# Layer norm of the last two batches with channels on the partitions: token statistics as rows by way of DRAM, in place of transposes on TensorE

## The reference

```python
xn = (x - mean(x)) / sqrt(var(x) + 1e-5)        # over the channels
q, k, v = xn @ wq.T, xn @ wk.T, xn @ wv.T       # 16 heads of q, 4 of k and v, 128 wide; rope on q and k
s = lightning_attention(q, k, v) @ wo.T         # linear attention with decay
h = silu((xn @ q8(gate_w)) * gate_scale) * ((xn @ q8(up_w)) * up_scale)    # 1536 wide, q8 rounds to fp8 e4m3
g = silu((h @ q8(down_w)) * down_scale)
out = x + s * g
```

## Time and profile before

| | us |
|---|---|
| three runs | 907.12, 908.81, 908.90; median 908.81 |
| profiled execution | 907.59 |
| its span | 905.8 (granted clock 0.999) |
| PE busy | 889.8, 98% of the span |
| DVE busy | 631.0, 70% |
| ACT busy | 421.7, 47% |
| POOL busy | 373.0, 41% |

### The profile page before, as it was taken

One profiled execution on the slowest core, in us unless ns is written; L12 is line 12 of the kernel. 1 busy time (PEld: TensorE's weight loads), 2 busy tenths in 40 slices (PEclk: granted clock), 3 DMA queues, 4 the chain that ended last, 5 costly groups with the idle time before them and its releaser, 6 DMA issues.

```text
span 905.8 us, 12411 instructions
## 1 busy us (share of the span) xinstructions
PE 889.8 (98%) x4104; PEld 738.4 (82%) x4104; DVE 631.0 (70%) x903; ACT 421.7 (47%) x709; POOL 373.0 (41%) x276
## 2 busy tenths in 40 slices
PE   5999999999999999999999999999999999999997
PEld 4888888888788888888888888888888888888886
DVE  7777652676753256766777867677767677788797
ACT  3633443443533446345464444464544554634542
POOL 1011112121222475535456455364454563553547
PEclk9999999999999999999999999999999999999999
DMA  6793304477750624414333413144243143364482
GB/s 213 222 360 115 105 12 152 150 256 288 289 219 29 209 93 137 177 33 154 138 118 140 178 67 140 52 182 185 81 162 123 39 171 141 102 236 152 156 266 76
DMA packets 51115, 138.55 MB, mean 153 GB/s; under 512 B 4224, under 2 KB 25344, under 8 KB 45696
## 3 DMA queue, kind: packets, MB, share of 16 engines
q1 hardware_dynamic: 51072, 138.00, 43.1%
HBM read 96.04 MB, written 41.94 MB: 152 GB/s over the span
## 4 chain that ended last, share of the span: by engine, by line
PE 85%; issue 5%; POOL 4%; DVE 3%; DMA 2%; ACT 1%; POOLq 0%; SPq 0%; DVEq 0%; ACTq 0%
PE bank L1268 84%; POOL d_r L1204 2%; POOL rot L1213 1%; DMA v_decayed<-vd_split 1%; PE bank L1315 1%; DMA stage<-in_x_nat 0%; DVE tail_sb L1110 0%; PE bank L1424 0%; DVE vd_split L882 0%; DVE d_sb L1013 0%; DVE tail_sb L1112 0%; ACT gout L547 0%; DVE tail_sb L1096 0%; DVE acc L1106 0%; DVE stats L772 0%
## 5 line engine op out<-in xcount | busy, mean ns | idle before, releaser
L1268 PE MATMUL bank<-xn,aw 128*128 128x512 f32 x960 | 229.2, 390 | 0.0
L1213 POOL TENSOR_TENSOR rot<-rot 128x512 f32<-128x512 f32 x80 | 126.8, 1585 | 235.2 <-DVE rot L1000 235.2
L1268 PEld LDWEIGHTS bank<-xn,aw 128*128 128x128 f32 x960 | 179.0, 188 | 37.4 <-issue 0.7
L1268 PE MATMUL bank<-o_r,ow 128*128 128x512 f32 (+1 forms) x792 | 186.2, 385 | 0.0
L1204 POOL TENSOR_TENSOR d_r<-d_sb,d_r 128x512 fp32r<-128x512 f32 x127 | 166.8, 1337 | 37.0 <-ACT d_r L691 36.9
L1268 PE MATMUL bank<-xn,gu_w 128*128 128x512 f32 x768 | 179.9, 389 | 0.0
L1268 PEld LDWEIGHTS bank<-xn,gu_w 128*128 128x128 f32 x768 | 144.1, 188 | 30.1
L1268 PEld LDWEIGHTS bank<-o_r,ow 128*128 128x128 f32 x792 | 144.4, 188 | 28.5
L999 DVE TENSOR_TENSOR rot<-bank,rope 128x512 f32<-128x512 f32 x80 | 55.2, 690 | 103.2 <-ACT rot L671 103.2
L670 ACT COPY rot<-bank 64x512 f32<-64x512 f32 x80 | 46.8, 585 | 155.1 <-PE bank L1268 154.8
L691 ACT CAST d_r<-d_sb 128x512 fp32r<-128x512 f32 x128 | 79.0, 621 | 84.0 <-DVE d_sb L1059 61.6
(11 more groups left out here) (82 smaller groups left out, 943.9 us busy)
## 6 DMA issues: line engine op xcount, KB each, us to landing
xn<-xn_split SPq DMA_DIRECT2D x15, 2048.0 KB, 7.7
v_decayed<-vd_split SPq DMA_DIRECT2D x32, 512.0 KB, 3.4
vd_r<-v_decayed SPq DMA_DIRECT2D x16, 1024.0 KB, 7.0
v_r<-v_split SPq DMA_DIRECT2D x16, 512.0 KB, 5.6
wst<-in_mlp_w SPq DMA_DIRECT2D x10, 768.0 KB, 5.4
xn_split<-xn SPq DMA_DIRECT2D x3, 2048.0 KB, 10.7
stage<-in_attn_w SPq DMA_DIRECT2D x4, 1280.0 KB, 6.0
stage<-in_x_nat SPq DMA_DIRECT2D x16, 256.0 KB, 4.7
```

What stands on the lines that cost most here:

```text
L1213: pool.tensor_tensor(rot1[:, r % RRING, :], rot1[:, r % RRING, :], rot2[:, r % RRING, :], ALU.add).then_inc(qk_sum, 1)
L1268: last = pe.matmul(dst, a, b, start=start and x == 0, stop=stop and x == len(pairs) - 1)
```

## The change

Batches 0 and 1 stay as they are. For batches 2 and 3 the natural tiles are still loaded and their statistics taken. The columns of mean and rstd are then written to DRAM as rows (`store_rows`: two DMAs, in which every 4-byte element goes to a place of its own), x is loaded again as four tiles of `x_t` (128 channels x 512 tokens, 256 KB each), and the two rows are read back, each to all 128 partitions (`load_rows`: two DMAs of 256 KB on the SBUF side). DVE subtracts the mean row and multiplies by the rstd row, two instructions for each of the 4 tiles; ACT rounds the high part and DVE subtracts the low one, as before but out of SBUF.

SP: store_rows(2) and load_rows(2) stand behind the last weight load; store_rows(3) stands in (2, 2), load_rows(3) in (2, 5). The natural tiles 14 and 15 are loaded once the first two turned tiles of batch 2 are used up. spill_last moves from (2, 8)..(2, 11) to (2, 10), (2, 11), (3, 0), (3, 1), and the attention weights' load from (2, 8) to (2, 10). DVE and ACT: the normalising of batch 2 moves from slabs 6 to 10 to slabs 10 and 11, that of batch 3 from (2, 2)..(2, 7) to (2, 7), (2, 8) and (2, 9).

```diff
+SPILL_AT = [(2, 10), (2, 11), (3, 0), (3, 1)]
+NAT = [i % XRING for i in range(3 * TT)] + [4, 5, 0, 1]
+TURNED = {2: [0, 1, 2, 3], 3: [2, 3, 4, 5]}
...
+        rows = gout[:, 0:2, :]
...
+            def store_rows(s):
+
+                sp.wait_ge(rstd_d, s + 2)
+                i0, i1 = s * TT, s * TT + TT
+                sp.dma_start(row_dram[s - 2, 0].rearrange("t p -> p t"), mv[:, i0:i1, 0], allow_slow_non_contiguous=True).then_inc(row_out, 16)
+                sp.dma_start(row_dram[s - 2, 1].rearrange("t p -> p t"), rstd[:, i0:i1], allow_slow_non_contiguous=True).then_inc(row_out, 16)
+                for k in range(KT):
...
+                    sp.dma_start(stage[:, TURNED[s][k], :], x_t[k, :, bass.ts(ORDER[s], S)]).then_inc(xt_in[k], 16)
+
+            def load_rows(s):
...
+                sp.wait_ge(row_out, 32 * (s - 1))
+                for r in range(2):
+                    row = row_dram[s - 2, r].rearrange("t p -> (t p)")
+                    sp.dma_start(rows[:, r, :], row.unsqueeze(0).broadcast_to([P, S])).then_inc(row_in, 16)
...
             for m in range(6, MT):
                 load_w(m)
+            store_rows(2)
+            load_rows(2)
             for i in range(3 * TT, 4 * TT):
                 load_x(i)
             spill_xn(2)
...
+            def norm_t_hi(s, k):
+
+                act.wait_ge(scaled, (s - 2) * KT + k + 1)
...
+                act.copy(xn_of(s)[:, 0, k, :], stage[:, TURNED[s][k], :]).then_inc(ln_hi, 1)
...
-                if m in (6, 7):
-                    norm(2 * TT + 2 * (m - 6))
-                    norm(2 * TT + 2 * (m - 6) + 1)
-                if 7 <= m < 7 + TT:
-                    norm_hi(2 * TT + m - 7)
+                if m in (MT - 2, MT - 1):
+                    norm_t_hi(2, 2 * (m - MT + 2))
+                    norm_t_hi(2, 2 * (m - MT + 2) + 1)
...
+            def norm_t(s, ks):
+
+                dve.wait_ge(row_in, 32 * (s - 1))
+                c = (s - 2) * KT
+                for k in ks:
+                    dve.wait_ge(xt_in[k], 16 * (s - 1))
+                    xt = stage[:, TURNED[s][k], :]
+                    dve.tensor_tensor(xt, xt, rows[:, 0, :], ALU.subtract).then_inc(centred, 1)
+                for k in ks:
+                    dve.wait_ge(centred, c + k + 1)
+                    xt = stage[:, TURNED[s][k], :]
+                    dve.tensor_tensor(xt, xt, rows[:, 1, :], ALU.mult).then_inc(scaled, 1)
...
-                if 7 <= m < 7 + TT:
-                    norm_lo(2 * TT + m - 7)
+                if m in (MT - 2, MT - 1):
+                    norm_t(2, (2 * (m - MT + 2), 2 * (m - MT + 2) + 1))
+                if m == MT - 1:
+                    norm_t_lo(2, 0)
+                    norm_t_lo(2, 1)
                 fuse(1, m)
+            norm_t_lo(2, 2)
+            norm_t_lo(2, 3)
...
-                    if s == 2 and LND <= m < LND + TT:
-                        norm_lo(3 * TT + m - LND)
+                    if s == 2 and m in (7, 8):
+                        norm_t(3, (2 * (m - 7), 2 * (m - 7) + 1))
+                    if s == 2 and m in (8, 9):
+                        norm_t_lo(3, 2 * (m - 8))
+                        norm_t_lo(3, 2 * (m - 8) + 1)
...
-                if 7 <= m < 7 + TT:
-                    ln_transpose(2 * TT + m - 7)
...
-                    if s == 2 and LND <= m < LND + TT:
-                        ln_transpose(3 * TT + m - LND)
```

More of the change, by code:

```diff
@@ L224, in attention_mlp_kernel @@
         floor_c = sem("floor_c"); newton = sem("newton"); rstd_d = sem("rstd_d")
+        row_out = sem("row_out"); row_in = sem("row_in"); xt_in = [sem(f"xt_in{k}") for k in range(KT)]; centred = sem("centred"); scaled = sem("scaled")
         normed = sem("normed"); ln_t = sem("ln_t"); ln_hi = sem("ln_hi"); ln_lo = sem("ln_lo")
@@ L255, in ln_ps @@
         def ln_ps(i):
-            return bank[i % TT] if i < 2 * TT else bank[7]
+            return bank[i % TT]
         def ready(m, down=False):
@@ L288, in load_x @@
             def load_x(i):
-                if i >= XRING:
-                    sp.wait_ge(ln_t, i - XRING + 1)
-                sp.dma_start(stage[:, i % XRING, :], x_nat[ORDER[i // TT], :, i % TT, :]).then_inc(x_in[i % XRING], 16)
+                if i >= 3 * TT + 2:
+                    sp.wait_ge(ln_lo, 2 * TT + NAT[i] + 1)
+                elif i >= 3 * TT:
+                    sp.wait_ge(stats_d, i - 1)
+                elif i >= XRING:
+                    sp.wait_ge(ln_t, i - XRING + 1)
+                sp.dma_start(stage[:, NAT[i], :], x_nat[ORDER[i // TT], :, i % TT, :]).then_inc(x_in[NAT[i]], 16)
+            def store_rows(s):
[4 more added lines that the diff above has]
+                for k in range(KT):
+                    if s == 2:
+                        sp.wait_ge(ln_t if k < 2 else stats_d, 2 * TT if k < 2 else 2 * TT + k - 1)
+                    else:
+                        sp.wait_ge(ln_lo if k < 2 else stats_d, 2 * TT + k + 3 if k < 2 else 3 * TT + k - 1)
+                    sp.dma_start(stage[:, TURNED[s][k], :], x_t[k, :, bass.ts(ORDER[s], S)]).then_inc(xt_in[k], 16)
+            def load_rows(s):
+                if s == 2:
+                    for r in range(2):
+                        sp.wait_ge(v_out[r], 32 * (2 * TT // VFIRST))
+                else:
+                    sp.wait_ge(gate_out, 16 * KT)
+                sp.wait_ge(row_out, 32 * (s - 1))
+                for r in range(2):
+                    row = row_dram[s - 2, r].rearrange("t p -> (t p)")
+                    sp.dma_start(rows[:, r, :], row.unsqueeze(0).broadcast_to([P, S])).then_inc(row_in, 16)
             def load_piece(q):
@@ L386, in _ @@
                         store_vd(*VD_AT[s, m])
+                    if s == 2 and m == 2:
+                        store_rows(3)
+                    if s == 2 and m == 5:
+                        load_rows(3)
                     if s == 2 and m in (3, 5, 7, 9):
                         fetch_v((m + 1) // 2)
[L389 to L392, removed]
+                    if (s, m) in SPILL_AT:
+                        spill_last(SPILL_AT.index((s, m)))
+                    if (s, m) == SPILL_AT[0]:
+                        sp.wait_ge(ln_lo, NB * TT)
                         sp.dma_start(stage[:, 0:PT, :], attn_w[0]).then_inc(aw_in, 16)
@@ L633, in _ @@
                         v_round(VT_AT[s, m])
-                    if s == 2 and m in (2, 3):
-                        norm(3 * TT + 2 * (m - 2))
-                        norm(3 * TT + 2 * (m - 2) + 1)
-                    if s == 2 and LND <= m < LND + TT:
-                        norm_hi(3 * TT + m - LND)
+                    if s == 2 and m in (7, 8):
+                        norm_t_hi(3, 2 * (m - 7))
+                        norm_t_hi(3, 2 * (m - 7) + 1)
                     if s == 3 and AW_FROM <= m < AW_FROM + PT:
@@ L770, in tile_stats @@
             def tile_stats(i):
-                dve.wait_ge(x_in[i % XRING], 16 * (i // XRING + 1))
-                dve.bn_stats(stats[:, i, :], stage[:, i % XRING, :]).then_inc(stats_d, 1)
+                dve.wait_ge(x_in[NAT[i]], 16 * (NAT[:i].count(NAT[i]) + 1))
+                dve.bn_stats(stats[:, i, :], stage[:, NAT[i], :]).then_inc(stats_d, 1)
             def mean_var(grp):
@@ L809, in norm_lo, with norm_t_lo @@
                 dve.tensor_tensor(lo, ln_ps(i)[:].rearrange("p (k c) -> p k c", k=KT), hi.bitcast(F32),
+                                  ALU.subtract).then_inc(ln_lo, 1)
+            def norm_t(s, ks):
[9 more added lines that the diff above has]
+                    dve.tensor_tensor(xt, xt, rows[:, 1, :], ALU.mult).then_inc(scaled, 1)
+            def norm_t_lo(s, k):
+                dve.wait_ge(ln_hi, s * TT + k + 1)
+                dve.tensor_tensor(xn_of(s)[:, 1, k, :], stage[:, TURNED[s][k], :], xn_of(s)[:, 0, k, :].bitcast(F32),
                                   ALU.subtract).then_inc(ln_lo, 1)
@@ L1301, in v_tile @@
                     pe.wait_ge(ln_lo, v + TT)
+                    pe.wait_ge(v_lo, v)
                 else:
```

13 lines of the change are left out of this document (5 added, 8 removed).

## The result

The changed kernel took 919.94 us, the median of 4 runs (918.18 to 920.50), against 908.41 for the kernel before in the same comparison: ratio 1.0131, 95% interval 1.0118 to 1.0143. It is 11.5 us slower. The forecast was 905.8, so the size, the sign and the range were all missed. The profiled execution took 920.5 us, the slowest of the four, with a span of 918.7; that of the kernel before was 0.8 us under its median, so the two traces lie 12.9 us apart.

A forecast was written before the change was run, and what follows sets the result against it. PE, busy 98% of the span, was taken as the bound. 907.59 - 3.5 (transposes) - 0.5 (old gates wait) + 1.0 (new stall) = 904.6 for the profiled execution; median 905.8 us, range 904.3 to 907.2.

The forecast's parts named there:

- Batch 3, the DMA side: Row stores and 1 MB of x_t added in (2, 2) fit its free DMA time, 3.7 us; lag taken as 0.
- What covers the new work of batch 2: Before slab 10, some 29 us cover batch 2's row stores and loads; 4 us per row store, nothing on the path.
- rival D: Rows come late for batches 2 and 3 if a 4-byte element takes 0.5 us; +4, 912.8 us; chance 0.04.
- Nothing to 2 us of lag, taken as 0.: Delay of the stores of decayed v, next in (2, 3), from row stores and x_t loads added in (2, 2).
- rival C: Side chain of ACT, DVE and landings becomes the bound by (3, 0): 6.5 us stall, +2.5, 911.3 us; chance 0.08.
- the signs set down beforehand: Right: row stores landing under 10 us, among others. Wrong: PE waiting over 2 us together for silu or v_rest, among others.
- The second term: v_rest(12) behind the gates of (3, 0), its preceding store now behind the weights' load: 0 us taken, up to 2.
- -3.5 us for the transposes: PE loses the 32 transposes of batches 2 and 3, 8 x 0.44 us on the chain: 3.5 us less.
- the start of batch 2 without a wait: DVE's last low half done at 147.65, 0.9 us before PE needs it; 0 taken, with 0 to 0.5.
- the gates of (3, 0): PE waits for ACT's gates in (3, 0): a stall of 1.0 us in place of 0.5 now.
- The forecast's engine part: DVE's added batch 3 work in (2, 7) to (2, 9) delays ACT's silus, giving a 1.0 us PE stall at the gates.
- The v for (2, 7): 0.5 MB of row loads before fetch_v(3) in (2, 5) delay this v by 1.5 us; DVE starts (2, 7) at 201.

The follow-up runs named there:

- e2: Kernel before with only the two 4-byte row stores of batch 3 added in (2, 2), read by nobody; 911.91 us, ratio 1.0041.
- e12: Changed kernel with rows packed into 4 DMAs of 8 pieces, and spill_last and weights' load moved late, to (3, 0) to (3, 3); 907.02 us, ratio 0.9992.
- e11: Changed kernel with rows packed into 4 DMAs of 8 pieces, without DVE's four mean subtractions for batch 3; 911.16 us, ratio 1.0031.
- e10: Changed kernel with packed rows, late spill and weights, batch 3's x_t loads in (2, 0), rows in (2, 1), norm_t in (2, 3), (2, 4); 904.27 us.
- e1: Changed kernel without the two row stores of batch 3, which then uses batch 2's rows; 912.93 us, ratio 1.0047.
- e4: Changed kernel with batch 3's two row stores issued by ACT on its own queue at the end of (2, 2); 920.36 us, ratio 1.0134.
- e13: Kernel before with two unread 2 KB stores added in (2, 2), each 128 pieces of 16 B; 908.00 us, ratio 0.9999.
- e8: Changed kernel with mean and rstd packed and turned by DVE, rows leaving as 4 DMAs of 8 pieces of 128 B; 912.16 us, ratio 1.0053.
- e3: Changed kernel without batch 3's four x_t loads (1 MB), row stores kept; 916.67 us, ratio 1.0086.
- e9: Changed kernel with packed rows, late spill and weights, batch 3 normalised in (2, 4), (2, 5), its rows read back in (2, 2); 908.70 us, ratio 1.0015.

## Why the prediction was wrong

**The step that failed** is "Batch 3, the DMA side", with the price put into it under "What covers the new work of batch 2". I took 4 us for a row store, with 6.3 (the scales, 128 pieces of 112 B) as the upper bound; it is 11, outside both ends. The bounds came from rows with as many pieces (v_split, 512 B each) or with small pieces (the scales), and neither has pieces of 4 B. What the Trainium skill says in the place quoted there (DMA: Bandwidth & Descriptors, Rules for kernel authors and Specifications), one descriptor for each element and a read-modify-write below 512 B, was the right warning. The traces agree with the first (1023 packets recorded for the 1024 elements of e2); no run here shows the second. I let the warning count only where the rows could come late (rival D), not where they stand in front of others. Rival D's measure, landing time over the pieces on an engine, gives 11 / 64 = 0.17 us, under its edge of 0.28, and batch 2 did not wait: rows issued at 102.0, read back from 114.5, DVE's norm_t at 130.6.

In (2, 2) the same 11 us met the stores of decayed v. I had found 3.7 us free in that window and "Nothing to 2 us of lag, taken as 0."; the next store was 13 us under way and ACT waited 12.6 us. From there the course was rival C's (given 0.08): ACT's lag beyond the slack of the banks. It put 6.5 us of stall; there were 11.2, and 4.1 of slow clock on top, a term that no case of mine had. The forecast looked at waits of PE and forgot that a wait of 5.2 us can also slow what follows. Of the signs set down beforehand, one of being right failed (row stores landed in under 10 us), and one of being wrong came: PE waited 10.4 us for silu and v_rest, against 2.

**The second term** was v_tile(13), "0, up to 2": 3.2 us and 1.7 of slow clock; without the row stores even 4.4 and 2.2. I had named the mechanism (the weights now stand in front of the store) and priced it by the slack of before, not by the slack that the lag of (2, 7) to (2, 9) left. The chain of before was misread as well: 217.55 in the earlier trace rows is where the late store begins, and it landed 8.16 later, at 225.7.

**Right were:** -3.5 us for the transposes (slabs 7 to 10 take 9.07 us each in the profile after, as forecast); the start of batch 2 without a wait (last low half done at 147.4, PE there at 147.9; two meetings with POOL behind 139, I had counted one and a margin of 0.9); and, in part, the gates of (3, 0) at 0.8 for 1.0. In the changed kernel that wait came behind ACT's 12.6 us for a store and two longer stalls, which the forecast did not have, so the number there is luck; but e12, with the 12.6 us gone, still has 0.6 there and 1.3 at the silus, behind DVE's norm_t as forecast. The forecast's engine part was right in kind and put 1.0 us where 1.9 stand. How much of the rest is DVE's list of 26 to 31 us is not separated: e11 takes a third of the new work away and shows at most 1 us, and e10 moves the loads along with the work. The v for (2, 7) came in e1 at 203.5 and not at 201, behind the row loads, where I had 1.5 us of delay counted.

## What to carry to other kernels

A small DMA is not priced by its bytes: look at its pieces, and measure one with the same size of piece. The price can be paid by whoever comes behind it, on any queue, and a free DMA engine in the profile does not show that the way is free. Turn 4-byte columns on chip first. When two moves each fit into the slack of a chain, check them together: the burst was free in the kernel before and cost 5 us behind a lag of 4. Allow for slow clock behind a forecast stall of PE of some us: here it was 1.6 to 2.9 us behind nine of eleven stalls of 2.8 to 5.3 us, and nothing behind the other two. A list that fits into its slabs on average can still hold up an engine that waits for it in order, as norm_t did. Put together, coarse rows gave 7.8 us back, the late burst 5.1 and the earlier place of batch 3's work and loads 2.7.

## What the runs showed of the hardware

- Two DMAs of 512 pieces of 4 B (2 KB each) from SBUF to DRAM land in 9.6 to 12.0 us. Until they have landed, what is issued behind them soon moves slowly: 26 GB/s in e2 from 183 to 187 where the kernel before moves 347, 98 in the changed kernel from 177.5 to 186. Issued from ACT (e4), they hold up SP's stores too.
- The engines are through with these pieces long before: in e2 1023 of them are recorded between 178 and 179, the engines' share is 0.00 from 179 to 181.4, and the stores land at 186.5 and 187.7.
- Two stores of 128 pieces of 16 B land in 2.9 and 3.6 us (e13), four of 8 pieces of 128 B in 4.5 to 5.6 us ahead of 1 MB of loads (e8).
- PE's start differed by up to 1.5 us between executions (30.61 to 32.13), in code common to all these kernels; not explained.
- After PE had been idle for 5.2 us the granted clock was at its lower level for 4.8 us. After idle of 5.3 (e11), 4.4 (e1), 3.6 (e4), 3.4 (e3), 3.2 (after) and three times 2.8 us (e2, e8, e9) the matmuls behind were slow in the same way; each of the nine cost 1.6 to 2.9 us. After 3.3 us of idle in e3 (at 215.71) and in e4 (at 218.52) they were not, nor after 2.3 us and less. So the length of the idle time alone does not decide it:

```profile
215.71 2.11 PE L1338 MATMUL bank<-xn,gu_w 128*128 128x512 f32 x8 [3.31 <-ACT f_all L578]
217.66 1.98 PE L1338 MATMUL bank<-fsplit,dn_w 128*128 128x512 f32 x8
```

```profile
195.83 3.68 PE L1348 MATMUL bank<-xn,gu_w 128*128 128x512 f32 x8 [2.81 <-ACT f_all L578]
199.35 2.01 PE L1348 MATMUL bank<-fsplit,dn_w 128*128 128x512 f32 x8
```

The first pair of rows is e3, the second e9.
